# Issuing attention's operand loads from the SP queue instead of GpSimd's

## The reference, cut to what matters

```
h   = layernorm(x)
q,k,v = split(h @ W_attn.T)                 # 16 heads of D = 8
s   = q @ k.T / sqrt(8) + slope * (j - i), only j <= i
y   = softmax(s) @ v
x   = x + y @ W_proj.T
```

## Time and profile before

| | us |
|---|---|
| median of 3 runs | 1781.46 (1780.94 to 1782.33) |
| the profiled execution, its own time | 1782.71 |
| its span in the trace | 1781.0 |
| PE busy | 1289.9 |
| DVE busy | 1214.9 |
| POOL busy | 1030.5 |
| ACT busy | 825.2 |
| loads of Q, 192 KB each, issue to landing | 4.1 |
| loads of K, 192 KB each, issue to landing | 4.9 |

### The profile page before, as it was taken

The page is one execution under the profiler, slowest core; times in us unless marked ns, Lnnn a source line. Parts: engine busy times, 40 slices in busy tenths (PEclk is TensorE's granted clock), DMA queues, the critical chain, the costliest instruction groups (busy, mean ns, idle before and its releaser), DMA issues. The chain is left out here.

```text
span 1781.0 us, 34332 instructions
## 1 busy us (share of the span) xinstructions
PE 1289.9 (72%) x8762; PEld 705.7 (40%) x8763; DVE 1214.9 (68%) x3716; ACT 825.2 (46%) x2009; POOL 1030.5 (58%) x1071
## 2 busy tenths in 40 slices
PE   2888888888888888559116266626279999999996
PEld 1333333333333333158006233316246556555654
DVE  2777777777777778457662279877766666666663
ACT  0356666555555656501202166643334444444443
POOL 4455555554555554234005368968158888888886
PEclk9999999998999999855557665555579999999999
DMA  4433322322332333145004300300413333333332
GB/s 99 138 79 79 85 78 77 81 83 69 77 86 77 77 84 81 55 169 200 5 9 113 79 30 24 126 6 24 171 30 42 42 42 42 41 41 43 41 42 35
DMA packets 79454, 124.66 MB, mean 70 GB/s; under 512 B 22976, under 2 KB 47232, under 8 KB 75312
## 3 DMA queue, kind: packets, MB, share of 16 engines
q0 software_dynamic: 45568, 59.38, 18.4%
q1 hardware_dynamic: 25792, 51.63, 8.6%
q10 hardware_dynamic: 8032, 12.93, 2.0%
HBM read 65.65 MB, written 57.68 MB: 69 GB/s over the span
## 5 line engine op out<-in xcount | busy, mean ns | idle before, releaser
L472 DVE TENSOR_REDUCE mx<-psS 128x1 f32<-128x384 f32 (+3 forms) x768 | 426.2, 597 | 164.4 <-PE psS L368 155.0
L532 ACT ACTIVATE probs<-psE 128x512 f32<-128x512 f32 (+2 forms) x768 | 362.5, 529 | 236.7 <-PE psE L383 227.1
L281 POOL TENSOR_SCALAR_AFFINE_SELECT probs<-probs 128x512 f32<-128x512 f32 x256 | 162.3, 641 | 236.4 <-ACT probs L532 236.1
L1935 POOL DMA_INDIRECT out<-ex_y,ex_idx x144 | 236.5, 1643 | 47.9 <-issue 43.0
L395 PE MATMUL psY<-probs,vaug 128*32 128x512 f32 (+3 forms) x2048 | 209.3, 473 | 42.7 <-POOL probs L281 42.6
L364 PE MATMUL psS<-maskq,identb 128*128 128x128 bf16 (+1 forms) x768 | 161.6, 254 | 54.5 <-DVE mx L472 49.9
L1926 POOL DMA_INDIRECT ex_xg<-expert_tab,ex_idx x144 | 142.2, 988 | 66.0 <-issue 41.8
L364 PEld LDWEIGHTS psS<-maskq,identb 128*128 128x128 bf16 x768 | 64.0, 98 | 245.4 <-DVE mx L472 186.7
L1909 DVE SCALAR_TENSOR_TENSOR ex_h<-ex_psG,ex_w,ex_up 128x352 f32<-128x352 f32 x144 | 84.0, 584 | 111.3 <-ACT ex_w L2010 107.1
L383 PE MATMUL psE<-qop,kop 63*128 63x512 bf16 (+3 forms) x1024 | 141.7, 309 | 2.7 <-ACT probs L532 2.7
L368 PE MATMUL psS<-kop,qop 61*128 61x128 bf16 (+3 forms) x1024 | 142.3, 317 | 0.0
(11 more groups left out here) (314 smaller groups left out, 2558.7 us busy)
## 6 DMA issues: line engine op xcount, KB each, us to landing
y_scr<-ysb SPq DMA_DIRECT2D x64, 256.0 KB, 2.0
qkv_scr<-parts POOLq DMA_DIRECT2D x32, 384.0 KB, 3.0
qop<-qkv_scr POOLq DMA_DIRECT2D x32, 192.0 KB, 4.1
kop<-qkv_scr POOLq DMA_DIRECT2D x32, 192.0 KB, 4.9
expert_tab<-table_rows SPq DMA_DIRECT2D x1, 4352.0 KB, 14.4
qop<-qkv_scr POOLq DMA_DIRECT2D x32, 128.0 KB, 4.9
kop<-qkv_scr POOLq DMA_DIRECT2D x32, 128.0 KB, 6.3
pj_num<-y_scr SPq DMA_DIRECT2D x16, 256.0 KB
```

What stands on the lines that cost most here:

```text
L281: pool.affine_select(diag, diag, [[0, HG], [1, P]], ALU.is_ge, 0.0, base=0, channel_multiplier=-1).then_inc(s_msk, 1)
L472: dve.tensor_reduce(mx[:, j, 2 * p + h0:2 * p + h0 + nh], psS[k % 3][:, 0:nh * w].rearrange("p (h k) -> p h k", h=nh), AX, ALU.max).then_i ...
L532: act.activation(probs[st % 2][j][:, 2 * p + h0:2 * p + h0 + nh, :].rearrange("p h q -> p (h q)"), psE[k % 3][:, 0:nh * W[j]], ACT.Exp).th ...
L1935: pool.indirect_dma_start(out, bass.IndirectOffsetOnAxis(ap=idx[t % 8][:], axis=0), y[m][:], None, compute_op=ALU.add).then_inc(s_sc[m], 16)
```

## The change

`place_q` and `place_k` no longer belong to POOL's program but are issued by SP. For batch 0 they stand behind SP's loads of the constants. For the others they stand in SP's step 2, behind the two max rows of that step and ahead of the output store: the wait for the old readers, the wait for the stored Q parts, six loads, the wait for the stored K parts, six loads. POOL keeps the splits, the stores of the parts, and the selects. The loads, their shapes, tiles and semaphore are as they were.

```
 @@ sync @@
+            sp.wait_ge(s_pw, 16)
+            place_q(sp, 0)
+            sp.wait_ge(s_pw, 32)
+            place_k(sp, 0)
+
             def step(n, b, st, last):
...
+                if st == 2 and not last:
+                    if not isinstance(b, int) or b:
+                        sp.wait_ge(s_er, EN * G * b)
+                    sp.wait_ge(s_pw, 32 * b + 48)
+                    place_q(sp, 1 - n)
+                    sp.wait_ge(s_pw, 32 * b + 64)
+                    place_k(sp, 1 - n)
 @@ gpsimd @@
             factors(1)
-            place_q(0, 0)
-            place_k(0, 0)
             clear_v(1)
...
-                    if st == 2 and more:
-                        place_q(1 - b % 2, b + 1)
                     if st == 3 and b + 2 < nb:
                         factors(b + 2)
                     clear_future(u, 0)
...
-                    if st == 2 and more:
-                        place_k(1 - b % 2, b + 1)
```

More of the change, by code:

```diff
@@ L160, in there, with place_q, place_k @@
             return not isinstance(u, int) or 0 <= u < G * nb
+        ROWS = ((0, 3), (24, 2), (40, 1))
+        def place_q(eng, n):
+            for row, k in ROWS:
+                for p in range(2):
+                    q_src = qkv_scr[n, 0, 0:k].rearrange("a (d c h) q -> c (a d) (h q)", d=D, c=2)[p]
+                    lo = HALF * p + row
+                    eng.dma_start(qop[n][lo:lo + 8 * k].rearrange("p h q -> p (h q)"), q_src).then_inc(s_op, 16)
+        def place_k(eng, n):
+            for row, k in ROWS:
+                for p in range(2):
+                    k_src = qkv_scr[n, 1, 3 - k].rearrange("(d c h) q -> c d (h q)", d=D, c=2)[p]
+                    lo = HALF * p + row
+                    eng.dma_start(kop[n][lo:lo + 8 * k].rearrange("p h q -> p (h q)"),
+                                  k_src.unsqueeze(0).to_broadcast([k, D, HH * T])).then_inc(s_op, 16)
         def half(tile, p, hi):
@@ L240, in keep_part @@
                 pool.dma_start(qkv_scr[n, s].rearrange("a p q -> p a q"), parts[s][:]).then_inc(s_pw, 16)
[L242 to L261, removed]
             def factors(b):
```

## The result

| | before | after |
|---|---|---|
| median, us (4 runs each) | 1781.20 (1778.79 to 1782.33) | 1838.15 (1835.06 to 1844.17) |
| the profiled execution, its own time | 1782.71 | 1835.06 |
| its span | 1781.0 | 1833.3 |
| POOL busy | 1030.5 | 927.6 |

After over before is 1.0329, with a 95% interval of 1.0305 to 1.0352: **57 us slower**. The direction and the range of the prediction held; its 1814 was 24 us too low. In some executions of a kernel PE idles 4.1 to 4.6 us ahead of each of five batches, 21 to 22 us in all, with nothing in the profile that ends it, and the ratios leave most such runs out. The page of after says first what did not matter: POOL lost a tenth of its busy time and PE is where it was as a share.

The account below looks back on a forecast made before the run. PE and DVE were taken to alternate at the limit, with room on POOL. 31 us at batch heads and 1.5 at the start, +33 us on the median of 1781.46, gave 1814 us (chance 0.60); range 1779 to 1865.

Parts of the forecast that it names:

- What POOL loses is worth nothing: Attention batches: POOL sheds 6.4 us of issues per batch, but its delay to PE is covered by 0.5 us; worth 0.
- SP's twelve issues cost nothing: SP's third step: twelve issues take 4.1 to 7.8 us, the next max rows still leave on time by 2.2 us; cost 0.
- SP's queue gives each load the same engines: Operand loads on SP: every load gets the same first engines, so 34 K packets of 8 KB queue on two, 11.5 us.
- The wait at a batch's head, 2.1 us: Head of each batch: operands land at 388.65 where PE wants them at 386.58; stall 2.1 us, low 1.1, high 5.7.
- The low end of 5.0 for Q: Q loads ahead of K: 5.0 us, from a stretch said to move the same bytes, giving a stall of 1.1 us.
- Fifteen batch changes: Attention: every one of 15 batch changes stalls PE 2.1 us, 31 us in all, low 16, high 85.
- Rival 3: Batch heads: PE's stands bring half-speed clock periods in half the batches, 44 us on top, about 1858 us; chance 0.14.
- Before the first batch, +1.5 us: Start: Q leaves earlier but K queues behind it, ready at 42.7 against 41.19; +1.5 us, low +0.5, high +5.1.
- Rival 1: Operand loads: SP's queue spreads K as POOL's does, batches lose nothing, start gains 5.9 us, 1775.6 us; chance 0.14.
- rival 2: Batch heads: same first engines, but faster packets or interleaved Q bring data in by 386.6 to 386.9; 1781 to 1785; chance 0.12.
- K landings of 10 us and more: K loads on SP: sign that the forecast is right; landings of 5 to 7 us without a wait would show it wrong.

Follow-up runs that it names:

- e6_start_pool: Changed kernel, but POOL issues the loads of batch 0 as before the change and SP all others; 1832.7 us, ratio 1.0268 to before.
- e7_start_both: Kernel before, but for the first batch SP issues Q and POOL K, both once the K store has landed; 1803.9 us, ratio 1.0067.
- e8_q_sp_late_start: Changed kernel with K loads back on POOL, Q on SP, and SP's first Q loads held until the K store; 1774.9 us, ratio 0.9944 to before.
- e1_q_only: Changed kernel with only the Q loads on SP and the K loads back on POOL; 1774.1 us, ratio 0.9945 to before.
- e9_k_16_spare: Changed kernel with the 16-row K pair loaded once more into an unread tile, PE waiting for it too; 1918.6 us, ratio 1.0794 to before.

## Why the prediction was right, and where its numbers were off

**What POOL loses is worth nothing: right.** PE's waits for POOL went from 42.6 us in 15 to 39.2 in 14, POOL's own waiting grew by 151 us.

**SP's twelve issues cost nothing: right.** 6.0 us, inside the 4.1 to 7.8 foreseen; the max rows left on time.

**SP's queue gives each load the same engines: right, and shown.** The share of 0.12 to 0.13 while PE stands is that of two of sixteen engines. Cutting the loads that begin with a 2 took the loss away without touching queue, place or bytes, and 16 packets more cost what one chain says. That these are the first engines no trace here shows, since the shares name none. The Trainium skill's rule on why a semaphore is incremented by 16 (DMA: Bandwidth & Descriptors) has this queue take the lowest-numbered engines; the 0.12 agrees with it in number. The sentence of the same page's section on issuing engines that speaks of sequencer time only did not hold here: moving the same loads cost 57 us.

**The wait at a batch's head, 2.1 us: mechanism right, size low.** It is 2.9 us. The packets were priced too high, if anything: 0.34 forecast, 0.31 to 0.33 measured. What was too low is the rest of the sum, the 5.5 us for Q and 1.6 for both ends: with 34 x 0.32 = 10.9 us for the K chain, the measured 19.7 us from the first Q issue leave 8.8 for them, not 7.1. The start points at the ends: there K has nothing ahead of it, and its 14.0 us less 10.9 leave 3.1 us for them, the double of the forecast. Then 5.7 us stay for Q, near the 5.5. This is an estimate, since in a batch other transfers run beside. (The low end of 5.0 for Q was misread: the stretch of the earlier trace rows moved 5.0 x 173 = 865 KB, more than Q's 786, so other transfers are in it.) PE's date, by contrast, was right: 16.5 us behind SP's first issue forecast, 16.4 measured.

**Fifteen batch changes: one too many.** The first batch is a longer one, 45.0 us after and 45.4 before, and its operands were in. The heads cost 40.8 us where the sum had 15 x 2.1 = 31.

**The clock: a rival's mechanism, in part.** The forecast priced a stand at its own length. PE's busy time for the same matmuls grew by 11.0 us in fourteen batches, with the granted clock over the stretch at 0.92 instead of 0.95. Between the two levels of 1.2 and 2.4 GHz that is 2 x 0.08 x 652.7 = 104 us at the lower one, before 2 x 0.05 x 608.1 = 61. The stretch behind the head shown above, the same place before, and the first batch of after and of before:

```profile
422.00:425.00 3.00, 3.00 (x24) 1.41 (x22) 1.17 (x3) 1.66 (x3) 0.00 (x0) 0.50 0.01 3
387.00:390.00 3.00, 2.97 (x40) 1.24 (x37) 2.08 (x7) 2.04 (x4) 0.26 (x1) 1.00 0.00 0
48.37:93.37 45.00, 36.85 (x220) 13.76 (x221) 31.60 (x73) 14.09 (x29) 12.00 (x15) 0.81 0.44 141
41.19:86.57 45.38, 37.62 (x220) 13.95 (x220) 31.57 (x73) 14.10 (x29) 18.32 (x26) 1.00 0.47 140
```

Right behind a stand of 3.26 us the clock was at the lower level for 3 us, and PE, busy all the time, did 24 matmuls where 40 were done in about the same place before. That batch had 0.93 and 37.63 us of busy time; the one ahead of it, at 0.96 as most before, had 36.25. So one such period more costs some 1.3 us. Of the 43 us added at the lower level, 17 (2 x 0.19 x 45.0) lie in the first batch, where they cost nothing: PE was busy for 36.85 us at 0.81, for 37.62 at 1.00. The other 26 are eight or nine periods, an estimated 10 to 12 us, which is the growth measured. Rival 3 had a half-speed period of 5.5 us added in half of the batches, 44 us; a quarter of that came. It did not grow when the stands did: with 7.9 us at each head PE was busy for 522.8 us, as in after. `e6_start_pool`, with waits like after's, had 520.8.

**Before the first batch, +1.5 us: the step that failed.** It was +7.2, more than the high end. The sum took K's date from Q's loads in the rings, 24.1 + 5.5, and held the K store at the 3.0 us of a store alone. But the Q loads, which leave 3 us earlier on SP, now run beside the K store and slowed it to 8.5 us, so that K was issued at 34.3, where the sum had its packets start at 29.6. The trace of before could not show it, since POOL issued Q behind its own store; that the Q loads would now run beside the K store could have been read from the order of the code. `e7_start_both` and `e8_q_sp_late_start` bear it out: with the loads behind it, the store takes 3.0 us. K's later date is 4.7 of the 5.7 us that were missed, 0.6 of it because PE's first instruction came later in this profile (13.52 for 12.91). The other 0.9 stand behind the issue, 14.0 us for the 11.5 + 1.6 of the sum.

In all: 40.8 for 31 at the heads (+9.8), 7.2 for 1.5 at the start (+5.7), 11.0 of clock less 2.9 us elsewhere in attention (+8.1), and 3.8 us less behind it, 20 of the 24 us by which 1838 is above 1814. The other 4 are between the profiled executions and the medians: after's is 3.1 below its own, before's 1.3 above the one that the forecast started from.

**Rival 1 (faster)** is out by the shares, **rival 2 (same)** by the waits. One sign named for the forecast, K landings of 10 us and more, could not be read: the profile lists no landing time for these loads on SP's queue. The small gain of `e1_q_only` is not explained by the trace: its fourteen batches are 3.9 us shorter than before's, less than the 5.5 us by which one batch of 48.20 us is long in before's profile, and 4.1 us of its gain lie behind the last x transposes, where only the last batch and code that was not changed still run. That it is faster, by some half a per cent, is measured; why is open.

## What to carry to other kernels

Before a load is moved from GpSimd's queue to SP's, look at the first dimension of its source: in this kernel loads with a repeat of 2 or 3 in front lay on the same few engines each time, and formed one chain of 0.32 us for each 8 KB. Cut them so that more engines share the rows, or leave them where they are, above all when they also start later than before; and count the time that a later operand has left by its last packet on the busiest engine, not by its issue. A transfer that may start earlier also runs beside something new: ask what that was, and whether the next step waits for it.

## What the runs showed of the chip beyond that

- A store of 384 KB that lands in 3.0 us alone took 8.5 us beside six loads, 768 KB in all, in another queue (3.0 again when these stood behind it). The Trainium skill's account of arbitration (DMA: Bandwidth & Descriptors, Queues, rings and completion order) has each engine take turns between the queues it has work for, packet by packet. The trace agrees in that the store is held up, and does not show the turns; the 5.5 us more are nearly the 6 us that the Q loads fill alone.
- SP needs 0.38 us to issue a Q load and 0.62 to issue a K load of the same size; POOL needs 0.52 and 0.56.
- From the first K issue to PE's first batch it took 10.9 to 11.1 us in three kernels as different as POOL's six loads, SP's eight and SP's twelve. What sets this floor was not found. On SP bytes start slowly: the first two us behind after's K issue moved them at 12 GB/s.
- Waits of 7.9 us ahead of each batch lowered the clock's mean over fourteen batches to 0.88, but PE's busy time stayed at 522.8 us. Part of the lower level fell into the stand: from 408 to 412 us, where PE did nothing, the clock of `e9_k_16_spare` stood at 0.50.
